# A drain in slots of two heads, and code passes, key norm and rescaling at other places of the step

## What is computed

```python
# cross attention: 16 heads of 32, 257 image keys and 12287 text keys
k = rms_norm(linear(ctx_txt, k_w, k_b), norm_k_w);  v = linear(ctx_txt, v_w, v_b)
txt_x = softmax(q @ k.T / sqrt(32)) @ v             # the same for the image keys, and added
x = x + linear(txt_x + img_x, o_w, o_b)
# self attention: 16 heads of 128, weights are codes * scales (64 tiles of 128x512)
x = x + self_attention(layernorm(x), wq_codes * wq_scales, ...)
# feed forward: 32 experts of which 4 are chosen for a row, and 1 shared
x = x + moe(layernorm(x))
```

## Time and profile before

| what | value |
|---|---|
| median of 3 runs | 1200.07 us (1199.26 to 1204.12) |
| the profiled execution, whole | 1197.79 us |
| its span, first to last instruction | 1196.1 us |
| PE busy | 1154.2 us (96%) |
| DVE, ACT, POOL busy | 947.6, 876.7 and 764.0 us |

### The profile page before, as it was taken

One profiled execution on the slowest core, in us unless ns is written; L12 is line 12 of the kernel. 1 busy time (PEld: TensorE's weight loads), 2 busy tenths in 40 slices (PEclk: granted clock), 3 DMA queues, 4 the chain that ended last, 5 costly groups with the idle time before them and its releaser, 6 DMA issues.

```text
span 1196.1 us, 26329 instructions
## 1 busy us (share of the span) xinstructions
PE 1154.2 (96%) x8794; PEld 950.5 (79%) x8794; DVE 947.6 (79%) x1611; ACT 876.7 (73%) x1891; POOL 764.0 (64%) x1064
## 2 busy tenths in 40 slices
PE   6999999999999999999999999999998879899998
PEld 4778888888888888888888888888887658588886
DVE  4778788887788787787878887778887778499997
ACT  5577877778777777777787777877777757388885
POOL 7988788887889788898887887888873000000000
PEclk9999999999999999999999999999999989899999
DMA  7135677665875657766667665686654899579990
GB/s 257 40 97 153 170 194 184 175 180 158 215 191 152 171 168 204 195 168 175 177 170 195 181 172 167 170 209 166 184 140 108 252 394 398 208 270 362 364 369 15
DMA packets 129327, 236.72 MB, mean 198 GB/s; under 512 B 15014, under 2 KB 42150, under 8 KB 128812
## 3 DMA queue, kind: packets, MB, share of 16 engines
q1 hardware_dynamic: 129196, 235.05, 66.5%
HBM read 140.87 MB, written 17.04 MB: 132 GB/s over the span
## 4 chain that ended last, share of the span: by engine, by line
PE 61%; POOL 11%; SPq 11%; DVE 6%; DMA 4%; issue 4%; ACT 2%; POOLq 0%; DVEq 0%; ACTq 0%
PE ps L1573 22%; PE ps L1437 12%; SPq L354 10%; PE ps L1599 5%; PE ps L1632 4%; DMA code_scale<-code_scales 3%; PE ps L1800 3%; PE ps L1803 3%; PE ps L1806 3%; POOL cx_blocks L624 2%; DVE small L1197 2%; POOL cx_blocks L622 2%; PE ps L1821 1%; PE ps L1829 1%; PE ps L1825 1%
## 5 line engine op out<-in xcount | busy, mean ns | idle before, releaser
L1573 PE MATMUL ps<-w_text,cx_blocks 128*128 128x512 f32 x1974 | 488.2, 394 | 0.5 <-ACT v_first L814 0.5
L1573 PEld LDWEIGHTS ps<-w_text,cx_blocks 128*128 128x128 f32 x1974 | 366.9, 188 | 86.8 <-issue 7.7
L857 ACT ACTIVATE p<-ps,small 128x512 f32<-128x512 f32 (+2 forms) x400 | 272.3, 682 | 116.7 <-DVE small L1199 112.8
L1197 DVE TENSOR_REDUCE small<-ps 128x1 f32<-128x512 f32 (+2 forms) x400 | 269.7, 674 | 87.4 <-PE ps L1599 86.9
L1437 PE MATMUL ps<-ident,p 128*128 128x128 f32 x1584 | 209.0, 273 | 11.0 <-DVE pt L1191 7.0
L1437 PEld LDWEIGHTS ps<-ident,p 128*128 128x128 f32 x1584 | 184.8, 141 | 41.2 <-issue 11.5
L839 ACT ACTIVATE pt<-ps 128x512 f32<-128x512 f32 (+1 forms) x296 | 164.4, 589 | 36.9 <-PE ps L1437 36.8
L622 POOL TENSOR_TENSOR cx_blocks<-cx_sum,small 128x256 fp32r<-128x256 f32 x188 | 119.1, 633 | 82.5 <-PE ps L1573 69.0
L624 POOL TENSOR_TENSOR cx_blocks<-cx_sum,cx_blocks 128x256 fp32r<-128x256 f32 x188 | 140.3, 746 | 14.7
L1599 PE MATMUL ps<-k_stack,q_stack 96*128 96x512 f32 (+1 forms) x400 | 146.2, 438 | 2.0 <-ACT p L857 1.7
L1199 DVE TENSOR_TENSOR small<-small 128x1 f32<-128x1 f32 x400 | 132.6, 331 | 13.7
(11 more groups left out here) (252 smaller groups left out, 1923.3 us busy)
## 6 DMA issues: line engine op xcount, KB each, us to landing
expert<-experts SPq DMA_DIRECT2D x34, 1536.0 KB, 8.7
k_stack<-kt_hi SPq DMA_DIRECT2D x384, 128.0 KB, 3.3
cx<-ctx_t SPq DMA_DIRECT2D x48, 512.0 KB, 5.0
k_stack<-kt_lo SPq DMA_DIRECT2D x192, 128.0 KB, 3.1
codes<-codes SPq DMA_DIRECT2D x64, 256.0 KB, 3.1
code_scale<-code_scales SPq DMA_DIRECT2D x64, 256.0 KB, 3.8
scaled<-codes SPq DMA_DIRECT2D x64, 256.0 KB, 2.3
weight_q<-scaled SPq DMA_DIRECT2D x1, 4096.0 KB, 15.3
```

What stands on the lines that cost most here:

```text
L857: eng.activation(pb[:, lo:hi], score_bank(s, h)[:, lo:hi], exp, bias=nm[1 - par][:, h:h + 1], accum_out=ls[1 - par][:, h:h + 1]).then_inc( ...
L1197: eng.tensor_reduce(ngm[:, h:h + 1], score_bank(s, h)[:, lo:hi], AX.X, ALU.max, negate=True).then_inc(e_gm, 1)
L1573: last = eng.matmul(ps_a[(p + i + 1) % 2][:, :], blk[:, i, a, c * P:(c + 1) * P], w_t[:, i, w, c * D:(c + 1) * D], start=(i in FRESH and c ...
```

## The change

- **POOL:** in the first half of a step the first code pass stands behind one more sum and split; the norm of key tile 3 stands between the two sums of the second half and not behind both; the second code pass stands behind `split_first(1)` and the norm of the next step's tile 0; the third stands at the end of the step.
- **SP:** the third pass of a step (`pass_codes(s, 1)`) stands behind the load and the 12 DMAs of `stack(0)`, ahead of the next step's `stack(1)`.
- **DVE:** `scale_attention` is cut in two: `scale_sums` in slot 1 and the scaling of `o_st` in slot 2, in place of slot 5.
- **Step 24, second half** (`drain_keys`): two heads at a time, tile 3 squared ahead of the split of tile 2, the split of tile 3 behind two more exponentials.
- **Step 25** (`drain`): two heads at a time; heads in the order 0, 4, 1, 5, 2, 6, 3, 7, 8 to 15, so that two in a row read the same part of `k_stack`; each head's exponential takes the group's own maximum as bias, and no line 1199 is run for it. One operation for all 16 heads brings the maxima together at the end (`last_differences`), one more exponential makes scales for this group's sums, and two more small multiplications use them. 10 of its 16 heads are stored by DVE (6 before). Values of heads 0 to 3 and 4 to 7 are weighed one right after the other, in slot 6.
- **Step 26** (`last_values`): an order of its own.

```diff
-        BY_DVE, BY_DVE_LAST = (0, 2, 8, 10), (0, 1, 7, 8, 10, 15)
+        BY_DVE = (0, 2, 8, 10)
+        BY_DVE_LAST = {NG - 2: (0, 2, 6, 8, 10, 12, 14), NG - 1: (0, 2, 4, 5, 6, 8, 10, 11, 12, 14)}
+        LAST_ORDER = (0, 4, 1, 5, 2, 6, 3, 7, 8, 9, 10, 11, 12, 13, 14, 15)
...
-                pass_codes(s, 1, m, loop)
                 if 1 <= s < NG:
                     load_next(s)
...
+                pass_codes(s, 1, m, loop)
...
                     split(0, 3, sum_x[:, :, :], 0)
+                    third_sum(0)
+                    split(0, 4, sum_x[:, :, :], 3)
                 scale_codes(s * W_STEP - (W_FIRST * W_STEP + 1), (m + 1) % 2, loop)
                 if strass:
-                    third_sum(0)
-                    split(0, 4, sum_x[:, :, :], 3)
                     fourth_sum(0)
...
-                    first_sums(1)
+                    first_sum(1)
                 if cur:
                     key_norm(s, 3, 1)
+                if nxt:
+                    second_sum(1)
                 if strass:
                     split(0, 6, quarter(0, 1, 1), 0)
-                scale_codes(s * W_STEP - W_FIRST * W_STEP, m % 2, loop)
...
# ACT, second half of step 24
+                def drain_keys(j):
+
+                    if j == 4:
+                        square_keys(s, 3, 1)
                         keys_high(s, 2, 1)
+                        store(g, 5)
+                    if j == 6:
+                        keys_high(s, 3, 1)
+                    exponential(2 * j)
+                    if j == 4:
+                        scale_keys(s, 3, 1)
+                    if j > 4:
+                        store(g, 2 * j - 3)
+                    exponential(2 * j + 1)
...
# DVE, step 25
+                def last_maximum(x):
+
+                    h = head_at(g, x)
+                    eng.wait_ge(e_qk, g * NH + x + 1)
+                    eng.tensor_reduce(ngm[:, h:h + 1], score_bank(s, x)[:, lo:hi], AX.X, ALU.max, negate=True).then_inc(e_gm, 1)
...
-                    if end and j == 5:
+                    if end and j == 1:
+                        scale_sums()
+                    if end and s < NG - 1 and j == 2:
                         scale_attention()
...
# PE, step 25
+                def drain(j):
+
+                    if j < 2:
+                        transpose_probabilities(g - 1, 2 * j + 12)
+                        transpose_probabilities(g - 1, 2 * j + 13)
+                    if j == 2:
+                        weigh_values(g - 1, 3 * HC - 1)
+                        weigh_values(g - 1, 4 * HC - 1)
+                    products_of_queries(2 * j)
+                    products_of_queries(2 * j + 1)
+                    if j == 6:
+                        weigh_values(g, HC - 1)
+                        weigh_values(g, 2 * HC - 1)
+                    if j >= 2:
+                        transpose_probabilities(g, 2 * j - 4)
+                        transpose_probabilities(g, 2 * j - 3)
```

More of the change, by code:

```diff
@@ L309, in stored_by_dve, with head_at @@
         def stored_by_dve(g, h):
-            return h in (BY_DVE if g < NG - 2 else BY_DVE_LAST)
+            return h in BY_DVE_LAST.get(g, BY_DVE)
+        def head_at(g, x):
+            return LAST_ORDER[x] if g == NG - 1 else x
         def stored(dve, g, h):
@@ L830, in step, with store @@
                     eng.wait_ge(e_wlo, 8)
-                def store(h, lag):
-                    gp, hp = behind(g, h, lag)
+                def store(gp, hp):
                     if not stored_by_dve(gp, hp) and (score if gp == g else end):
@@ L887, in slot @@
                     for h in (2 * j, 2 * j + 1):
-                        store(h, LAG)
+                        store(*behind(g, h, LAG))
                     if end and j == 2:
@@ L1613, in weigh_values @@
                 def weigh_values(gp, hp):
+                    at = [head_at(gp, x) for x in range(NH)].index(hp)
                     for dve, e in ((True, e_pte), (False, e_pta)):
-                        eng.wait_ge(e, stored(dve, gp, hp))
+                        eng.wait_ge(e, stored(dve, gp, at))
                     if hp == HC - 1:
@@ L1633, in weigh_values @@
                                               vb[k][:, head * HD:(head + 1) * HD],
-                                              pt_sb[head % NPT][:, k * P:(k + 1) * P],
+                                              pt_sb[[head_at(gp, x) for x in range(NH)].index(head) % NPT][:, k * P:(k + 1) * P],
                                               start=(k == 0), stop=(k == nk - 1))
@@ L1687, in step @@
+                for j in range(SLOTS if s <= NG else 0):
+                    if s == NG:
+                        drain(j)
+                    elif draining(s, 2 * j):
+                        drain_keys(j)
                     else:
                         slot(j)
+                if s == NG + 1:
+                    last_values()
             steps(eng, step)
```

189 lines of the change are left out of this document (121 added, 68 removed).

## The result

| | before | after |
|---|---|---|
| median of 4 runs, us | 1199.66 | 1218.4 |
| the profiled execution, us | 1197.79 | 1213.52 |
| its span, us | 1196.1 | 1211.8 |

The ratio of the times is 1.0149, with a 95% interval of 1.010 to 1.0199. The forecast was 1191 us, with a range up to 1202: the change makes the kernel slower by 12 to 24 us, and the forecast missed in sign. The loss lies in the steady steps.

What follows compares the result with a forecast made beforehand. PE's matmul issue, 36.33 us a step, was taken as the floor, with waits for key tiles and exponentials above it. Steady steps -8.0 and drain -1.3 make -9.3 us, from 1200.07 to 1191 us; range 1185 to 1202.

Steps and rivals of the forecast that it cites:

- Third pass at the end of the step ... cost 0: Steady steps: POOL waits for the late pass's scales at the next step's start, but tile 1's norm has cover; cost 0.
- The cover was 3.9 us and 1.0 us of it is left: Steady steps: spare time between tile 1's norm being ready and ACT scaling that tile, before and after the move.
- POOL catches up by the second split, since it waited there for PE anyway: Steady steps: POOL's delay from the third pass at the step's head is absorbed by its existing waits for PE.
- the forecast's own signs of being wrong: Steady steps: PE waits for exponentials in most steps, ACT waits for tile 1's norm, or scales land over 5 us after issue.
- SP. Cost 0: SP queue, steady steps: a load goes out earlier, stack(1) is 1.5 us later but read only in slot 4; cost 0.
- The norm of tile 3, -6.5 us: Steady steps: the norm comes 1.35 us earlier, so PE's 6.8 us of waits for scaled key tiles nearly go; -6.5 us.
- The rescaling, -2.5 us: DVE, steady steps: moving it to slots 1 and 2 removes part of PE's 4.1 us wait for exponentials; -2.5 us.
- New collisions, +1.0 us: Steady steps: allowance for new collisions and other small waits, between 0 and 5 us, taken as +1.0 us.
- the second rival: DVE, slots 1 and 2: POOL blocks the moved small operations, giving back 6.6 us; 1197 to 1198 us, chance 0.14.
- The steady sum, -8.0 us: All steady steps: -6.5 for key tiles, -2.5 for the rescaling, +1.0 for collisions; -8.0 us, bounds -11 and +3.
- The drain, -1.3 us: Drain: head 11's score 1.7 us earlier, 0.4 us more from there to the final sum; -1.3 us, bounds -4.5 and +2.5.
- After the drain, cost 0: Second layer's weights: weight_k's load has 3.4 us of cover, of which 1.3 + 0.7 are used; cost 0.
- The third rival: Head of each steady step: POOL waits for the third pass's scales beyond tile 1's cover; 1208 us, chance 0.08.

Runs made afterwards that it cites:

- e3: Kernel before with only the third code pass moved to the step's end, on both SP and POOL: 1228.81 us, ratio 1.0208 to the kernel before.
- e8: Kernel before with only POOL's third code pass moved to the step's end, SP's left in place: 1202.39 us, ratio 1.0004 to the kernel before.
- e10: Changed kernel with only POOL's second code pass put back ahead of the second pair's first split: 1220.28 us, ratio 1.0167 to the kernel before.
- e12: Changed kernel with POOL's second pass and SP's third pass put back, POOL's third still last in the step: 1186.98 us, ratio 0.9881 to before.
- e9: Changed kernel with only POOL's third pass moved into the next step, behind the norm of key tile 2: 1197.73 us, ratio 0.9983 to before.
- e11: The changed kernel itself, run again beside e9 and e10 on one chip: 1222.88 us, ratio 1.0176 to the kernel before.
- e1: Changed kernel with the third code pass put back on both SP and POOL, POOL's second pass still late: 1253.23 us, ratio 1.0428 to before.
- e7: Kernel before with the changed drain and norm order (first pass late), rescaling in slot 5: 1191.56 us, ratio 0.9902 to before.
- e4: Kernel before with only the changed drain; passes, norm order and rescaling as before: 1199.15 us, ratio 0.9969 to the kernel before.
- e5: Kernel before with the changed drain and the rescaling in slots 1 and 2: 1203.57 us, ratio 1.0007 to the kernel before.
- e6: Changed kernel with POOL's second pass put back and the third back on both SP and POOL: 1186.48 us, ratio 0.9864 to the kernel before.

## Why the prediction was wrong

**The step that failed: "Third pass at the end of the step ... cost 0".** It has three parts.

*"in my estimate until 4.6 us after alpha (issue 0.3 to 0.7 us after alpha, 4.3 us or so on the way as in the earlier trace rows)".* POOL began at 5.7 to 7.8 us in 20 of 21 steps, and at 4.5 us only in the quick one. The issue is at 0.2 to 2.0 us, and the way is 5.0 to 6.4 us in these 20. The load of the earlier trace rows was itself 4.5 us on the way, and it came from another place: one stack and a load of context ahead of it, and no stack right behind it. Here 12 DMAs stand ahead and 12 behind.

*"The cover was 3.9 us and 1.0 us of it is left".* True of tile 1 at 4.6 us; at 5.7 to 7.8 it is overdrawn by 0.1 to 2.2 us, and ACT waited for this norm, up to 3.7 us. Of PE's waits this accounts for the smaller part, the 6.5 us at the transposes.

*"POOL catches up by the second split, since it waited there for PE anyway".* This is the worst of the three, since it hid tile 3. In the step of before from 420.29 POOL waited for PE twice ahead of the first pass:

```profile
429.70 0.62 POOL L622 TENSOR_TENSOR cx_blocks<-cx_sum,small 128x256 fp32r<-128x256 f32 x1 [1.02 <-PE ps L1573]
...
432.86 0.62 POOL L622 TENSOR_TENSOR cx_blocks<-cx_sum,small 128x256 fp32r<-128x256 f32 x1 [1.74 <-PE ps L1573]
```

That is 2.76 us, with 0.61 us more for scales behind them. The pass at the head puts 1.29 us and a wait in front. With the forecast's wait of 2.5 us it is 3.8 us, already a little over this store; with the measured 4.2 us it is 5.5 us, 2 us over. After the change POOL waited for PE for 20.4 us in the 22 steps instead of 67.9, and in the step from 503.58 not once ahead of tile 3's norm. The 2 us ate the 1.35 us by which the norm should have come earlier, and more: in the median step it starts 23.1 us after alpha, before 22.3. I had checked the moved work against the next consumer only, tile 1, and not summed what lay between it and tile 3.

e3 and e8 show it in the kernel before, e10 and e12 in the changed one: each pair differs only in SP's place for the pass, and that place costs 25 to 34 us, where the forecast had 0. The landing is not the whole of it. In e9 POOL asks late enough, and 0.0193, 23 us, come back against e11; some 12 us are left, of the kind that follows. Two of the forecast's own signs of being wrong came true, ACT's wait for the norm of tile 1 and landings later than 5 us after issue.

**"SP. Cost 0".** It was wrong in two ways, neither seen in the sum. The pass between the stacks delays the scales, and when that is hidden, the second stack holds ACT (e9). And its place is not free to choose: it has to stand behind POOL's second pass (e1).

**The other terms.** *The norm of tile 3, -6.5 us:* e7 against e4 gives 8.0 us, and the wait for keys is gone; right. *The rescaling, -2.5 us:* with the norm early it is 4.6 us, alone nothing. The mechanism was right, and the sums of e4 and e5 fit the remark that cured steps enter the next wait. *New collisions, +1.0 us,* and the second rival: they did not come. The second small operation of the rescaling, as a group in e6 (slot 1) and in e7 (slot 5), 89 to 900 us, and one of each with POOL's operation beside it, in the last two blocks:

```profile
L1269 DVE TENSOR_TENSOR small<-small x22: 174/176/178, 97.7 to 864.7; 128x16 f32<-128x16 f32 x22
```

```profile
L1269 DVE TENSOR_TENSOR small<-small x22: 175/406/709, 117.3 to 887.5; 128x16 f32<-128x16 f32 x22
```

```profile
426.73 0.17 DVE L1269 TENSOR_TENSOR small<-small 128x16 f32<-128x16 f32 x1
...
427.21 0.62 POOL L632 TENSOR_TENSOR cx_blocks<-cx_sum,small 128x256 fp32r<-128x256 f32 x1 [1.30 <-PE ps L1657]
```

```profile
446.34 0.71 DVE L1269 TENSOR_TENSOR small<-small 128x16 f32<-128x16 f32 x1
...
446.28 0.73 POOL L634 TENSOR_TENSOR cx_blocks<-cx_sum,cx_blocks 128x256 fp32r<-128x256 f32 x1
```

In slot 5 it meets POOL, is held to 0.71 us and ends with POOL's operation (447.05 and 447.01 us); in slot 1 it falls into the 1.3 us in which POOL waits for PE, and none of the 22 rows is over 178 ns. The rule of the Trainium skill that I weighed ("SBUF — State Buffer", "Who interferes with whom") agrees with the slot 5 row; it had spoken for the move, not against it, since it asks what runs at that very moment and I had asked which of POOL's operations are large. *The steady sum, -8.0 us:* e6 has (892.50 - 89.29) / 22 = 36.51 us a step in its trace, 7.5 us less than before, and by the ratios e6 lies 0.0105, 12.6 us, below e4. The trace agrees with the sum, and by the ratios the sum was too small by a third; e6's profiled execution was one of its two slowest.

*The drain, -1.3 us.* Timeline of the kernel after, steps 24 and 25, DVE, PE and DVE (answers to the earlier trace rows):

```profile
945.62 0.69 DVE L1117 TENSOR_TENSOR kt_lo<-ps,kt_hi 128x512 fp32r<-128x512 f32 x1
...
964.56 0.84 PE L1683 MATMUL ps<-k_stack,q_stack 96*128 96x512 f32 x2
...
979.18 0.56 DVE L1294 TENSOR_TENSOR o_st<-ps,small 128x384 f32<-128x384 f32 x1
```

From alpha of step 24 to the final sum it took 979.18 - 918.39 = 60.8 us, before 962.76 - 900.02 = 62.7 us: 1.9 us won. Head 11's score, the second of the pair at 964.56, is at about 964.9, 46.5 us after that alpha (before 48.5): 2.0 us won, where I had 1.7. That this is so near is in part luck. The low part of tile 3 was ready at 946.31, 1.9 us later in its step than before, where I had 0.7; from there to the score it took 18.6 us, where I had 20.0. From the score to the end 14.3 us, as before, where I had 0.4 us more. By e4 the drain gives 3.7 us, within the bounds. A single execution says little here: from the alpha of step 24 to the final sum the nine traces with the changed drain took 57.8 to 63.0 us, the longest in e11, the same kernel again, and the three with the old one (before, e3, e8) 62.2 to 66.5 us. In one stretch of the changed kernel's drain the granted clock fell (windows of the kernel after: us, busy time by engine, granted clock, DMA share, GB/s):

```profile
954.00:959.00 5.00, 5.00 (x70) 3.70 (x69) 1.44 (x3) 2.31 (x7) 1.27 (x1) 0.53 0.92 223
```

PE waited for stores twice between 948.6 and 952.3 and was then granted 0.53 of its clock, about its lower level of 1.2 GHz, for 5 us (the next stretch has 1.00 again); the value products of the group before ran in it, and VectorE waited 3.2 us for the score behind them. That this cost time in the end is not shown: e11's drain was granted 1.00 from 949 to 990 us and took 63.0 us, e9's had 1.00 from 915 to 956 us and took 60.3 us. The kernel before had such a stretch too, with 0.57 from 940 to 944 us.

*After the drain, cost 0.* `weight_k` is issued at 971.66 and lands 25.4 us later, at about 997; ACT read it at once and had waited 1.2 us for it. The 3.4 us of cover are used up, since the load is issued 974.34 - 971.66 = 2.7 us before the last alpha, where it was 958.35 - 952.4 = 5.9. The stretch behind the final sum is 232.6 us, against 233.3: no loss in the end.

**The rivals.** The third rival is what happened. Its deciding point, 1.0 us later than thought, fits the profile; its chance of 0.08 and its price were too small. I priced it at 0.8 us a step on top of the forecast, 1208 us, for 2.5 us of lateness. POOL was 1.1 to 3.2 us late, and the price by e3 against e8 is 1.1 us a step, by e10 against e12 1.6 us. It was priced by tile 1 alone, and most of it came by tile 3. What spoke for the rival stood in the forecast: one step with 4.6 us from issue to start, and DMAs of two stacks around the new place. A landing read at another place of the queue was taken as the landing here.

## What to carry to other kernels

When a wait for a transfer is moved in front of other work, take its duration from several transfers at a place of the queue with the same traffic on both sides, reckon with the longest of them, and add delay plus work up to every consumer behind it on that engine, against the idle time that lies before each; the first consumer's cover says nothing of the third's. Where two queues share a pass (one loads and stores, one computes), their places can be moved apart only as far as the stores still find their tile ready: in e12 POOL alone went late at no cost, in e1 SP went ahead of what it had to store, and the stack behind it paid. Of two small waits in one loop, curing one may only feed the other: try them together before one is called useless.

## What the runs showed of the hardware

The same load of scales, 256 KB, took 3.0 us in the median from issue to landing with no stack beside it. Between two stacks of 12 DMAs of 128 KB each it took 5.0 to 6.4 us in 20 steps of the kernel after and 3.7 us in one, with the 16 DMA engines 96% busy around one of these loads, that of 543.34; windows of the kernel after:

```profile
541.00:550.00 9.00, 9.00 (x104) 7.49 (x103) 7.41 (x16) 6.90 (x18) 4.76 (x7) 1.00 0.96 231
```

The longest of e10's were 6.6 us in the step from 390.22, 7.2 us in the one from 429.48 and 7.6 us in the one from 733.36, where POOL idled 5.92 us. In the kernel after, the last DMA of the stack ahead had landed at most 1.4 us after the load's issue in each of these steps, and the scales landed 2.1 to 3.4 us behind the codes (1.1 us in the quick step), against 0.6 to 0.8 us with no stack beside them. The same POOL pass took 1.28 to 1.30 us in all of these places.
